# A DLRM forward pass on one core: MLP layers a pair per round ahead, the last pair gathered by halves, nine by-hand pairs

## The chip, the core and the metric

The kernel runs on one core of a Trainium2 chip. The metric is the device time of one launch in microseconds (us), the median of three runs. The core has five engines that run their own instruction streams and meet at semaphores: PE (matrix products; PEld is its weight load), DVE (vector work), ACT (scalar work, here mostly a DMA queue), POOL (here it issues the gathers) and SP (a DMA queue).

## The reference, cut to what matters

There are 2048 samples, 13 dense features, 26 tables of 12500 rows of 64 float32, an MLP 13-512-256-64 and a last layer of 256 outputs.

```python
x = jax.nn.relu(dense_features @ W0 + b0)
x = jax.nn.relu(x @ W1 + b1)
dense_out = jax.nn.relu(x @ W2 + b2)
emb = jax.vmap(lambda t, idx: t[idx], in_axes=(0, 1), out_axes=1)(tables, sparse_features)
gram = jnp.einsum('bid,bjd->bij', emb, emb)
interact = gram[:, TRIU_I, TRIU_J]
features = jnp.concatenate([dense_out, interact], axis=1)
return features @ Wt + bt
```

An index is clamped to its table (and a negative one wraps) before it is used.

## The kernel before

**Tiling.** The samples are cut into 32 units of 64, and two units (u = 0, 1) make a pair of 128 samples; there are 16 pairs, m = 0 to 15. Two pairs are a round (8 rounds), and the MLP is computed once per round on 256 samples.

**Gathers (POOL, `gather`, L276).** A gather is one indirect DMA of 128 rows of 256 bytes: two neighbouring fields (slot k of 13) of the 64 samples of one unit. A pair has 13 slots in two units, 26 gathers, in four chunks of 4, 4, 4 and 1 slots (`CHUNKS`). `emb` holds three pairs (`PR = 3`), so the gathers of pair m wait until the transposes of pair m-3 are done.

**By-hand rows (`fetch_rows`, L209).** In the eight pairs of `BY_HAND` one slot (`HAND_K` = 11) isn't gathered by POOL: its 256 rows are fetched by as many plain DMAs of one row each, those of unit 0 on SP's queue and those of unit 1 on ACT's, 32 at a time after a load of 32 row offsets into registers (a "piece"). SP fetches pair after pair. ACT has its pieces in a fixed order with the stores of the outputs in between: `store(done)` stands ahead of piece `done * 7 // 3 + 6` and waits for that output.

**A pair on PE and DVE.** PE transposes each chunk's rows (`transposes`, L506), DVE copies them to `embT` (`embT_evac`, L354). PE then makes the products of 4 samples at a time in two halves of 16 matmuls (`gram_products`, L524), into one PSUM tile, so that a half must be copied out (`gram_blocks`, L361, 16 copies of DVE) before the next is written. `top` (L542) multiplies the MLP's output and the products by the last layer's weights, DVE copies the result (`out_evac`, L391), and ACT stores it. In the last pair half of the 16 copies of a half are ACT's (`ACT_BLOCKS`).

**The order** is written out by hand, in `tensor_round` (L557) and `vector_round` (L398). In a round r the first layer (`mlp_l0`) stands behind the products of pair 2r, the second and third (`mlp_l1`, `mlp_l2`) between and behind the products of pair 2r+1. In the last round all three layers and `top(14)` stand ahead of the transposes of pair 15:

```python
                    mlp_l1(r)
                    mlp_l2(r)
                    top(2 * r)
                    transposes(2 * r + 1)
                    gram_products(2 * r + 1, 0)
                    gram_products(2 * r + 1, 1)
```

Of the kernel before, what the change touches and what calls it, by code (L numbers as in the profile page):

```python
# [5 lines left out]
def bass_dlrm_forward(  # L6
# [15 lines left out]
    i32 = mybir.dt.int32  # L22
# [38 lines left out]
    BY_HAND = [2, 4, 6, 8, 9, 11, 13, 15]  # L61
    HAND_K = 11
    LOADED = 32
    ROW = EMB * 4

# [19 lines left out]
    with ctx:  # L85
# [26 lines left out]
        row_idx = sb("row_idx", [P, NU, NK], u32)  # L112
        emb = sb("emb", [P, PR, NK, 2, EMB])
# [17 lines left out]
        h2 = sb("h2", [H2 + 1, RS])  # L131
# [14 lines left out]
        later_ready = sem("later_ready")  # L146
        hand_idx_in = sem("hand_idx_in")
# [47 lines left out]
        LAST_PAIR = NP - 1  # L195
# [69 lines left out]
        def _(pool):  # L265
# [29 lines left out]
            for m in range(NP):  # L295
                gather(m)

        @block.vector
        def _(dve):
# [49 lines left out]
            nc.vector.memset(h2[H2:H2 + 1, :], 1.0).then_inc(consts_set, 1)  # L349
            nc.vector.memset(w_tri[:, :, :], 0.0).then_inc(tri_zeroed, 1)  # L350
# [47 lines left out]
            def vector_round(r):  # L398
                embT_evac(2 * r)
                gram_blocks(2 * r, 0)  # L400
                if r > 0:
                    out_evac(2 * r - 1)
                gram_blocks(2 * r, 1)
                l0_evac(r)
                if r < ROUNDS - 1:
                    embT_evac(2 * r + 1)
                    gram_blocks(2 * r + 1, 0)
                    l1_evac(r)
                    gram_blocks(2 * r + 1, 1)
                    l2_evac(r)  # L410
                    out_evac(2 * r)
                else:
                    l1_evac(r)
                    l2_evac(r)
                    out_evac(2 * r)
                    embT_evac(2 * r + 1)
                    gram_blocks(2 * r + 1, 0)
                    gram_blocks(2 * r + 1, 1)

            dve.wait_ge(mlp_w_in, 96)  # L420
            for r in range(ROUNDS):
                vector_round(r)
# [3 lines left out]
        def _(act):  # L426
# [3 lines left out]
            with nc.allow_non_contiguous_dma(reason="bias columns"):  # L430
                act.dma_start(b0_sb[:, :], b0.rearrange("(c p) -> p c", p=P)).then_inc(mlp_w_in, 16)
                act.dma_start(b1_sb[:, :], b1.rearrange("(c p) -> p c", p=P)).then_inc(mlp_w_in, 16)
                act.dma_start(b2_sb[:, :], b2.rearrange("(p c) -> p c", c=1)).then_inc(mlp_w_in, 16)

# [12 lines left out]
            for i, (m, c0) in enumerate(pieces):  # L447
                for done in range(LAST_PAIR):
                    if done * 7 // 3 + 6 == i:
                        store(done)  # L450
                fetch_rows(act, 1, m, c0, c0 + LOADED)
            for done in range(LAST_PAIR):
                if done * 7 // 3 + 6 >= len(pieces):
                    store(done)
# [8 lines left out]
        def _(pe):  # L463
# [35 lines left out]
            def mlp_l2(r):  # L499
# [4 lines left out]
                last.then_inc(l2_in_psum, 1)  # L504

# [18 lines left out]
            def gram_products(m, half):  # L524
# [7 lines left out]
                pe.wait_ge(embT_ready[LAST], m + 1)  # L532
# [9 lines left out]
            def top(m):  # L542
                q = m % 2
                pe.wait_ge(h2_ready, m // 2 + 1)
                nc.tensor.matmul(mlp_ps[q][:, 0:NO], h2[:, q * P:(q + 1) * P], wd_sb[:, :], start=True, stop=False)  # L545
# [11 lines left out]
            def tensor_round(r):  # L557
                transposes(2 * r)
                gram_products(2 * r, 0)
                if r > 0:  # L560
                    top(2 * r - 1)
                gram_products(2 * r, 1)
                mlp_l0(r)
                if r < ROUNDS - 1:
                    transposes(2 * r + 1)
                    gram_products(2 * r + 1, 0)
                    mlp_l1(r)
                    gram_products(2 * r + 1, 1)
                    mlp_l2(r)
                    if r == 0:  # L570

                        pe.wait_ge(w_top_in, 96)
                        pe.wait_ge(tri_zeroed, 1)
                    top(2 * r)
                else:
                    mlp_l1(r)
                    mlp_l2(r)
                    top(2 * r)
                    transposes(2 * r + 1)
                    gram_products(2 * r + 1, 0)  # L580
                    gram_products(2 * r + 1, 1)

            for r in range(ROUNDS):
                tensor_round(r)
# [28 lines left out]
```

## Time and profile before

| | us |
|---|---|
| median of 3 runs (lowest, highest) | 541.34 (540.68, 541.42) |
| the profiled execution, own time | 541.29 |
| its span in the trace | 539.5 |
| PE busy in the span | 296.8 |
| DVE busy | 255.4 |
| POOL busy | 378.7 |

The profiled execution lies within the three runs; what lies around its span is 1.8 us. An engine's busy time counts only what its unit works, not what its sequencer does: POOL's gaps between two gathers are time in which nothing is waited for.

### The profile page before, as it was taken

The page shows a single profiled execution, that of the slowest core. Times are in us where ns is not written, and L with a number is a line of the kernel's source. Part 1 is how long each engine was busy: PE and PEld are TensorE (multiplying, and loading weights), DVE is VectorE, ACT ScalarE, POOL GpSimd, SP SyncE. Part 2 cuts the span into 40 slices and gives each one's busy share as a digit, 9 for nine tenths or more (in the row PEclk, how much of TensorE's full clock was granted, in tenths as well). Part 3 has the DMA queues.
Part 4 walks back from the last instruction along what each step waited for, and adds up shares of the span by engine and source line. Part 5 has one row for each costly group of instructions (what it writes and reads, how often), then busy time and mean ns, then how long its engine had stood idle before and what let it go on. Part 6 is the DMA issues. An engine that isn't in the chain of part 4 may idle for free.

```text
span 539.5 us, 8990 instructions
## 1 busy us (share of the span) xinstructions
PE 296.8 (55%) x1728; PEld 236.3 (44%) x1728; DVE 255.4 (47%) x656; ACT 8.7 (2%) x21; POOL 378.7 (70%) x407
## 2 busy tenths in 40 slices
PE   2015545861867517574366927529176381858666
PEld 1014334750645416463344815428064261647455
DVE  4404618471545716346182454525554273555442
ACT  2000000000000000000000000000000000000011
POOL 5777777777777777777777777777777777777300
PEclk9555558865576757767587666777577675878696
DMA  5212224122222223233232323232232322222000
GB/s 104 29 28 30 32 48 88 39 28 37 30 29 39 27 29 39 29 37 30 38 30 28 37 28 39 30 38 29 28 38 29 39 29 37 30 37 37 15 11 11
DMA packets 24758, 18.73 MB, mean 35 GB/s; under 512 B 14455, under 2 KB 18265, under 8 KB 24684
## 3 DMA queue, kind: packets, MB, share of 16 engines
q0 software_dynamic: 12800, 13.13, 17.6%
q1 hardware_dynamic: 6356, 2.49, 4.3%
q10 hardware_dynamic: 5546, 2.53, 4.1%
q14 instruction: 42, 0.34, 0.2%
q8 instruction: 14, 0.23, 0.2%
HBM read 15.20 MB, written 2.10 MB: 32 GB/s over the span
## 4 chain that ended last, share of the span: by engine, by line
POOL 61%; issue 21%; PE 7%; DVE 6%; DMA 3%; ACT 0%; POOLq 0%; DVEq 0%; ACTq 0%
POOL emb L288 61%; DVE gram L203 4%; PE gram_ps L538 3%; DMA emb<-in_L_rec_tables_dram,row_idx 3%; PE mlp_ps L553 2%; DVE embT L188 1%; PE mlp_ps L495 1%; DVE h L371 1%; DMA raw_idx<-n_r_sparse_features_dram 0%; ACT gram L203 0%; PE mlp_ps L545 0%; DVE out_sb L396 0%; PE rowsT_ps L520 0%; PE mlp_ps L502 0%; DVE wrap L315 0%
## 5 line engine op out<-in xcount | busy, mean ns | idle before, releaser
L288 POOL DMA_INDIRECT emb<-in_L_rec_tables_dram,row_idx x400 | 378.0, 945 | 125.6 <-issue 121.8
L203 DVE COPY gram<-gram_ps 32x96 f32<-32x96 f32 x496 | 161.0, 325 | 96.0 <-PE gram_ps L538 88.2
L520 PE MATMUL rowsT_ps<-ident,emb 128*128 128x128 f32 x200 | 43.7, 349 | 163.2 <-DMA emb<-in_L_rec_tables_dram,row_idx 160.2
L538 PE MATMUL gram_ps<-embT 64*128 64x100 f32 x1024 | 92.8, 350 | 29.3 <-DVE gram L203 17.1
L520 PEld LDWEIGHTS rowsT_ps<-ident,emb 128*128 128x128 f32 x200 | 28.7, 174 | 179.3 <-issue 178.5
L188 DVE COPY embT<-rowsT_ps 128x512 f32<-128x512 f32 x64 | 52.5, 851 | 115.3 <-PE rowsT_ps L520 114.4
L538 PEld LDWEIGHTS gram_ps<-embT 64*128 64x128 f32 x1024 | 86.9, 259 | 38.5 <-issue 38.5
L553 PE MATMUL mlp_ps<-w_gram,gram 128*128 128x256 f32 x224 | 75.9, 512 | 1.7 <-DVE gram L203 1.7
L553 PEld LDWEIGHTS mlp_ps<-w_gram,gram 128*128 128x128 f32 x224 | 61.8, 276 | 17.0 <-DVE gram L203 2.4
L495 PE MATMUL mlp_ps<-h,w_sb 128*128 128x256 f32 x128 | 38.9, 470 | 3.5 <-DVE h L371 3.5
L545 PE MATMUL mlp_ps<-wd_sb,h 65*128 65x256 f32 x32 | 17.9, 660 | 35.7 <-DVE h L371 35.7
L495 PEld LDWEIGHTS mlp_ps<-h,w_sb 128*128 128x128 f32 x128 | 30.3, 244 | 10.8 <-DVE h L371 4.2
L396 DVE COPY out_sb<-mlp_ps 128x256 f32<-128x256 f32 x16 | 6.8, 425 | 55.7 <-PE mlp_ps L553 55.4
L371 DVE TENSOR_SCALAR h<-mlp_ps,b_sb 128x256 f32<-128x256 f32 (+1 forms) x56 | 24.1, 477 | 7.8 <-PE mlp_ps L495 5.9
L545 PEld LDWEIGHTS mlp_ps<-wd_sb,h 65*128 65x128 f32 x32 | 7.4, 287 | 40.6 <-DVE h L371 33.9
L487 PE MATMUL mlp_ps<-xT,w_sb 13*128 13x256 f32 x64 | 21.3, 485 | 0.0
L487 PEld LDWEIGHTS mlp_ps<-xT,w_sb 13*128 13x128 f32 x64 | 14.5, 237 | 3.6 <-issue 0.5
L203 ACT COPY gram<-gram_ps 32x96 f32<-32x96 f32 (+1 forms) x16 | 5.2, 322 | 516.7 <-PE gram_ps L538 516.5
L502 PE MATMUL mlp_ps<-h,w_sb 128*64 128x256 f32 x32 | 8.6, 392 | 1.0 <-DVE h L371 1.0
L472 PE MATMUL rowsT_ps<-ident,x_sb 128*13 128x128 f32 x16 | 3.6, 412 | 5.6 <-DMA x_sb<-in_r_dense_features_dram 5.6
L350 DVE MEMSET w_tri<- 32x6400 f32 x1 | 5.4, 5392 | 1.4 <-issue 1.4
L502 PEld LDWEIGHTS mlp_ps<-h,w_sb 128*64 128x64 f32 x32 | 3.7, 136 | 3.3 <-DVE h L371 1.4
(25 smaller groups left out, 17.3 us busy)
## 6 DMA issues: line engine op xcount, KB each, us to landing
by_hand<-in_L_rec_tables_dram SPq DMA_DIRECT2D x1024, 0.2 KB
by_hand<-in_L_rec_tables_dram ACTq DMA_DIRECT2D x1024, 0.2 KB
emb<-in_L_rec_tables_dram,row_idx POOLq DMA_INDIRECT x400, 3.4
out_dram<-out_sb ACTq DMA_DIRECT2D x16, 128.0 KB, 6.7
w_gram<-w_tri SPq DMA_DIRECT2D x3, 192.0 KB
w_sb<-in_L_rec_W_dram SPq DMA_DIRECT2D x1, 512.0 KB
raw_idx<-n_r_sparse_features_dram SPq DMA_DIRECT2D x2, 182.0 KB, 4.1
w_gram<-w_tri SPq DMA_DIRECT2D x1, 224.0 KB
```

The lines of the kernel that those rows point to most:

```text
L188: return copy(embT[:, m % 2, :, 0:F].rearrange("p s (k x) -> p k x s", x=2)[:, ks.start:ks.stop], rowsT_ps[c % 2][:, 0:len(ks)])
L203: last = copy(by_quad[FP * g:FP * (g + 1), t0:NS, :, half * HG:(half + 1) * HG, s], gram_ps[FP * s:FP * (s + 1), :, :, src:src + SQ * (NS ...
L288: nc.gpsimd.indirect_dma_start(emb[:, m % PR, k, u, :], None, tables_v[:, :], bass.IndirectOffsetOnAxis(ap=row_idx[:, 2 * m + u, k:k + 1], ...
L371: return nc.vector.tensor_scalar(out, in_, bias, 0.0, ALU.add, ALU.max)
L396: nc.vector.tensor_copy(out_sb[:, q, :], mlp_ps[q][:, 0:NO]).then_inc(out_ready[q], 1)
L487: last = nc.tensor.matmul(mlp_ps[half][:, m * RS:(m + 1) * RS], w0_sb[:, c * P:(c + 1) * P], xT[:, bass.ds(r * 2, 2), :], start=True, stop ...
L495: last = nc.tensor.matmul(mlp_ps[0][:, m * RS:(m + 1) * RS], w1_sb[:, c, m * P:(m + 1) * P], h0[:, c, :], start=(c == 0), stop=(c == H0 // ...
L502: last = nc.tensor.matmul(mlp_ps[1][0:H2, 0:RS], w2_sb[:, c, :], h1[:, c, :], start=(c == 0), stop=(c == H1 // P - 1))
L520: last = nc.tensor.transpose(rowsT_ps[c % 2][:, k - ks.start, :, :], rows.rearrange("p u e -> p (u e)"), ident[:, :])
L538: last = nc.tensor.matmul(gram_ps[:, u, a, 0:SQ * (F - 1)], samples.rearrange("p s f -> p (s f)"), samples[:, :, 1:F], start=True, stop=True)
L545: nc.tensor.matmul(mlp_ps[q][:, 0:NO], h2[:, q * P:(q + 1) * P], wd_sb[:, :], start=True, stop=False)
L553: last = nc.tensor.matmul(mlp_ps[q][:, 0:NO], gram[:, q, t, :], w_gram[:, t, :], start=False, stop=(t == NS - 1))
```

## The change

1. The MLP of all rounds moves forward and stands in one piece: round 0's ahead of pair 0, and round m+1's behind the products of pair m, for m = 0 to 6. `h2` holds all rounds. The zeroing of `w_tri` (5.4 us on DVE) moves behind the first MLP.
2. The last pair is gathered otherwise: four fields of 32 samples in a gather, so that the first 12 gathers hold the first half of each unit's samples and the next 12 the second half. Its indices come by eight small DMAs on ACT's queue at the start and 14 small DVE operations behind pair 1. Transposes, copies and products of the first half stand ahead of those of the second.
3. Groups of 4, 3 and 5 spare products on PE, which nobody reads, stand between the last pair's steps.
4. Nine by-hand pairs in place of eight, at other places, with slot 12 in place of 11; for the last pair the by-hand rows are a chunk of their own (`None`), the third of six. A store stands one piece later on ACT's queue.

```diff
-    BY_HAND = [2, 4, 6, 8, 9, 11, 13, 15]
-    HAND_K = 11
+    BY_HAND = [2, 4, 5, 7, 9, 10, 12, 14, 15]
+    HAND_K = NK - 1
+    LAST_PAIR = NP - 1
+    LK = 2 * HAND_K // SQ
+    HS = US // 2
+    LAST_CHUNKS = [(0, 0, 4), (0, 4, LK), None, (1, 0, 4), (1, 4, 5), (1, 5, LK)]
+    HALF_DONE = [3, 6]
+    SPARE = [4, 3, 5]
...
+        def last_rowsT_evac(copy, i):
+            if LAST_CHUNKS[i] is None:
+                return copy(embT[:, LAST_PAIR % 2, :, 2 * HAND_K:F].rearrange("p s x -> p x s"),
+                            rowsT_ps[i % 2][:, 0, :, :])
+            half, k0, k1 = LAST_CHUNKS[i]
+            return copy(embT[:, LAST_PAIR % 2, half * HS:(half + 1) * HS, SQ * k0:SQ * k1].rearrange(
+                            "p s (k x) -> p k x s", x=SQ),
+                        rowsT_ps[i % 2][:, 0:k1 - k0].rearrange("p k y (x s) -> p k (y x) s", s=HS))
...
-            for m in range(NP):
+            for m in range(LAST_PAIR):
                 gather(m)
+            pool.wait_ge(rowsT_in_psum[LAST], LAST_PAIR + 1 - PR)
+            pool.wait_ge(last_idx_ready, 1)
...
+                for k in range(k0, k1):
+                    for u in range(2):
+                        nc.gpsimd.indirect_dma_start(
+                            emb[:, LAST_PAIR % PR, half * LK + k, u, :], None, tables_v[:, :],
+                            bass.IndirectOffsetOnAxis(ap=last_idx[:, half * 2 + u, k:k + 1], axis=0),
+                        ).then_inc(last_rows_in[i], 16)
...
             dve.wait_ge(mlp_w_in, 96)
-            for r in range(ROUNDS):
-                vector_round(r)
+            mlp_evac(0)
+            nc.vector.memset(w_tri[:, :, :], 0.0).then_inc(tri_zeroed, 1)
+            for m in range(LAST_PAIR):
+                embT_evac(m)
+                gram_blocks(m, 0)
+                if m > 0:
+                    out_evac(m - 1)
+                gram_blocks(m, 1)
+                if m + 1 < ROUNDS:
+                    mlp_evac(m + 1)
+                if m == 1:
+                    last_index()
+            dve.wait_ge(gram_in_psum, (LAST_PAIR - 1) * 2)
+            for i in range(HALF_DONE[0]):
+                dve.wait_ge(last_rowsT_in_psum, i + 1)
+                last_rowsT_evac(nc.vector.tensor_copy, i).then_inc(last_embT_ready, 1)
+            out_evac(LAST_PAIR - 1)
+            gram_blocks(LAST_PAIR, 0)
+            for i in range(HALF_DONE[0], HALF_DONE[1]):
+                dve.wait_ge(last_rowsT_in_psum, i + 1)
+                last_rowsT_evac(nc.vector.tensor_copy, i).then_inc(last_embT_ready, 1)
+            gram_blocks(LAST_PAIR, 1)
             out_evac(LAST_PAIR)
...
+            for x in range(SQ):
+                for a in range(2):
+                    act.dma_start(last_raw[x * HS:(x + 1) * HS, 2 * a:2 * a + 2, :],
+                                  sparse_v[a * HS:(a + 1) * HS, :, LAST_PAIR, :]).then_inc(last_idx_in, 16)
...
-                    if done * 7 // 3 + 6 == i:
+                    if done * 7 // 3 + 7 == i:
...
+            def spare(n):
+                pe.wait_ge(out_ready[(LAST_PAIR - 1) % 2], (LAST_PAIR - 1) // 2 + 1)
+                for _ in range(n):
+                    nc.tensor.matmul(mlp_ps[(LAST_PAIR - 1) % 2][:, 0:NO], ident[:, :], w_gram[:, 0, :], start=True, stop=True)
```

`last_transposes(i)` transposes chunk i of `LAST_CHUNKS` (for `None` the by-hand rows) into `rowsT_ps[i % 2]` once its rows have landed and the copy of chunk i-2 is done.

**PE at the end.** Before, from the products of pair 14's second half to the end of the program; L487, L495 and L502 are the MLP's layers, L545 and L553 are `top`, L520 transposes, L538 products:

```order
156 L538 MATMUL gram_ps<-embT 128x100 x16
157 L487 MATMUL mlp_ps0<-xT,w0_sb 128x256 x2
158 L487 MATMUL mlp_ps1<-xT,w0_sb 128x256 x2
159 L495 MATMUL mlp_ps0<-h0,w1_sb 128x256 x8
160 L502 MATMUL mlp_ps1<-h1,w2_sb 64x256 x2
161 L545 MATMUL mlp_ps0<-wd_sb,h2 128x256
162 L553 MATMUL mlp_ps0<-w_gram,gram 128x256 x7
163 L520 MATMUL rowsT_ps_0<-ident,emb 128x128 x4
164 L520 MATMUL rowsT_ps_1<-ident,emb 128x128 x4
165 L520 MATMUL rowsT_ps_0<-ident,emb 128x128 x3
166 L520 MATMUL rowsT_ps_0<-ident,by_hand 128x128
167 L520 MATMUL rowsT_ps_1<-ident,emb 128x128
```

In the changed kernel, from the same products on (L597 are the last pair's transposes, L605 spare products, L650 and L658 `top`, L642 products):

```order
153 L642 MATMUL gram_ps<-embT 128x100 x16
154 L597 MATMUL rowsT_ps_0<-ident,emb 128x128 x4
155 L597 MATMUL rowsT_ps_1<-ident,emb 128x128 x2
156 L650 MATMUL mlp_ps0<-wd_sb,h2 128x256
157 L658 MATMUL mlp_ps0<-w_gram,gram 128x256 x7
158 L597 MATMUL rowsT_ps_0<-ident,by_hand 128x128
159 L642 MATMUL gram_ps<-embT 128x100 x16
160 L597 MATMUL rowsT_ps_1<-ident,emb 128x128 x4
161 L605 MATMUL mlp_ps0<-w_gram,ident 128x256 x4
162 L597 MATMUL rowsT_ps_0<-ident,emb 128x128
163 L605 MATMUL mlp_ps0<-w_gram,ident 128x256 x3
164 L597 MATMUL rowsT_ps_1<-ident,emb 128x128
```

The MLP is gone from between pair 14 and pair 15, the transposes of the first half stand ahead of `top(14)`, and the by-hand chunk, behind `top(14)`, is ahead of the first half's products. Behind these rows stand the second half's products, five spare ones and `top(15)`.

**ACT at the end.** Before, the last pieces (L213 loads 32 offsets, L219 fetches 32 rows) and stores (L441):

```order
80 L441 DMA out_0_dram<-out_sb 128x256
81 L213 TENSOR_LOAD hand_off
82 L219 DMA by_hand<-in_L0_rec_tables_dram 1x256 x32
83 L213 TENSOR_LOAD hand_off
84 L219 DMA by_hand<-in_L0_rec_tables_dram 1x256 x32
85 L441 DMA out_0_dram<-out_sb 128x256
86 L213 TENSOR_LOAD hand_off
87 L219 DMA by_hand<-in_L0_rec_tables_dram 1x256 x32
88 L441 DMA out_0_dram<-out_sb 128x256 x3
```

In the changed kernel (L242, L248 and L514 are the same three):

```order
88 L514 DMA out_0_dram<-out_sb 128x256
89 L242 TENSOR_LOAD hand_off
90 L248 DMA by_hand<-in_L0_rec_tables_dram 1x256 x32
91 L242 TENSOR_LOAD hand_off
92 L248 DMA by_hand<-in_L0_rec_tables_dram 1x256 x32
93 L242 TENSOR_LOAD hand_off
94 L248 DMA by_hand<-in_L0_rec_tables_dram 1x256 x32
95 L514 DMA out_0_dram<-out_sb 128x256
96 L242 TENSOR_LOAD hand_off
97 L248 DMA by_hand<-in_L0_rec_tables_dram 1x256 x32
98 L514 DMA out_0_dram<-out_sb 128x256 x2
```

There are 36 pieces in place of 32, and 13 stores stand ahead of the last piece in both; two stores in place of three follow it.

## Rows read from the trace of the kernel before

**Rows 1.** The page: shares of the chain that ended last.

```profile
POOL 61%; issue 21%; PE 7%; DVE 6%; DMA 3%; ACT 0%; POOLq 0%; DVEq 0%; ACTq 0%
```

**Rows 2.** The chain's end in order of time: start, us, what.

```profile
441.86 16.20 DMA emb<-in_L_rec_tables_dram,row_idx
...
502.44 1.67 DVE h L371 x4
```

**Rows 3.** Groups of instructions, and POOL's last gather: start, us, idle before.

```profile
L288 POOL DMA_INDIRECT emb<-in_L_rec_tables_dram,row_idx x400 | 378.0, 945 | 125.6 <-issue 121.8
...
504.26 0.94 POOL L288 DMA_INDIRECT emb<-in_L_rec_tables_dram,row_idx  x1 [0.30 <-issue]
```

**Rows 4.** Gathers' landing in windows 90:100, 225:260, 320:360, 433:443, 463:475.

```profile
DMA to landing us min/median/max: 2.9/3.0/3.1
DMA to landing us min/median/max: 3.3/7.3/8.0
DMA to landing us min/median/max: 3.4/8.8/14.2
DMA to landing us min/median/max: 3.4/9.8/16.2
DMA to landing us min/median/max: 2.7/2.7/2.8
```

**Rows 5.** SP's and ACT's queues in order of time: start, us, what.

```profile
88.36 351.51 SPq L219 DMA_DIRECT2D by_hand<-in_L_rec_tables_dram  x896
...
4.38 0.50 ACTq L433 DMA_DIRECT2D b_sb<-in_L_rec_b_dram  x1
...
12.83 78.82 ACTq L219 DMA_DIRECT2D by_hand<-in_L_rec_tables_dram  x192
...
100.31 0.39 ACTq L441 DMA_DIRECT2D out_dram<-out_sb  x1
...
130.46 23.91 ACTq L219 DMA_DIRECT2D by_hand<-in_L_rec_tables_dram  x64
...
162.14 0.38 ACTq L441 DMA_DIRECT2D out_dram<-out_sb  x1
...
446.59 0.38 ACTq L441 DMA_DIRECT2D out_dram<-out_sb  x1
...
449.49 10.53 ACTq L219 DMA_DIRECT2D by_hand<-in_L_rec_tables_dram  x32
```

**Rows 6.** PE and DVE in order of time: start, us, shapes, idle before and releaser.

```profile
448.79 1.08 PE L520 MATMUL rowsT_ps<-ident,emb 128*128 128x128 f32 x4 [6.12 <-DMA emb<-in_L_rec_tables_dram,row_idx]
...
449.91 1.01 DVE L188 COPY embT<-rowsT_ps 128x512 f32<-128x512 f32 x1 [1.66 <-PE rowsT_ps L520]
...
459.15 3.74 PE L538 MATMUL gram_ps<-embT 64*128 64x100 f32 x32 [0.51 <-DVE embT L188]
...
468.57 2.03 PE L538 MATMUL gram_ps<-embT 64*128 64x100 f32 x32 [1.60 <-DVE gram L203]
...
470.71 5.37 DVE L203 COPY gram<-gram_ps 32x96 f32<-32x96 f32 x16 [1.38 <-PE gram_ps L538]
...
477.66 4.74 PE L553 MATMUL mlp_ps<-w_gram,gram 128*128 128x256 f32 x14
...
512.96 3.19 PE L553 MATMUL mlp_ps<-w_gram,gram 128*128 128x256 f32 x14
...
522.09 2.64 DVE L203 COPY gram<-gram_ps 32x96 f32<-32x96 f32 x8 [2.24 <-PE gram_ps L538]
...
525.11 3.73 PE L538 MATMUL gram_ps<-embT 64*128 64x100 f32 x32 [3.13 <-ACT gram L203]
...
531.71 5.09 PE L553 MATMUL mlp_ps<-w_gram,gram 128*128 128x256 f32 x14 [1.71 <-DVE gram L203]
...
536.84 0.42 DVE L396 COPY out_sb<-mlp_ps 128x256 f32<-128x256 f32 x1 [5.20 <-PE mlp_ps L553]
```

**Rows 7.** Window 525.2:535.3: length, busy PE, PEld, DVE, ACT, POOL; granted clock, DMA, GB/s.

```profile
525.20:535.30 10.10, 8.39 (x43) 6.76 (x44) 2.59 (x8) 2.60 (x8) 0.00 (x0) 0.50 0.01 2
```

More of the change, by code:

```diff
@@ L146, in bass_dlrm_forward @@
         later_ready = sem("later_ready")
+        last_idx_in = sem("last_idx_in")
+        last_idx_ready = sem("last_idx_ready")
+        last_rows_in = [sem(f"last_rows_in_{i}") for i in range(len(LAST_CHUNKS))]
+        last_rowsT_in_psum = sem("last_rowsT_in_psum")
+        last_embT_ready = sem("last_embT_ready")
         hand_idx_in = sem("hand_idx_in")
@@ L420, in _, with mlp_evac, last_index @@
-            dve.wait_ge(mlp_w_in, 96)
-            for r in range(ROUNDS):
-                vector_round(r)
+            def mlp_evac(r):
+                l0_evac(r)
+                l1_evac(r)
+                l2_evac(r)
+            def last_index():
+                dve.wait_ge(last_idx_in, 128)
+                for x in range(SQ):
+                    rows, raw = slice(x * HS, (x + 1) * HS), last_raw[x * HS:(x + 1) * HS, :, x:SQ * LK:SQ]
+                    nc.vector.tensor_scalar(last_wrap[rows], raw, 0.0, float(VOCAB), ALU.is_lt, ALU.mult)
+                    last = nc.vector.tensor_scalar(last_capped[rows], raw, float(VOCAB - 1), None, ALU.min)
+                last.then_inc(hand_idx_step, 1)
+                dve.wait_ge(hand_idx_step, 4)
+                nc.vector.tensor_tensor(last_wrapped[:, :, :], last_capped[:, :, :], last_wrap[:, :, :],
+                                        ALU.add).then_inc(hand_idx_step, 1)
+                dve.wait_ge(hand_idx_step, 5)
+                nc.vector.scalar_tensor_tensor(
+                    out=last_row[:, :, :], in0=last_wrapped[:, :, :], scalar=0.0,
+                    in1=field_base[:, :, 0:2 * LK:2].to_broadcast([P, 4, LK]), op0=ALU.max,
+                    op1=ALU.add).then_inc(hand_idx_step, 1)
+                dve.wait_ge(hand_idx_step, 6)
+                for x in range(SQ):
+                    rows = slice(x * HS, (x + 1) * HS)
+                    last = nc.vector.tensor_scalar(last_idx[rows], last_row[rows], float((x - x // 2) * VOCAB), None,
+                                                   ALU.add)
+                last.then_inc(last_idx_ready, 1)
@@ L504, in mlp_l2, with last_transposes @@
                 last.then_inc(l2_in_psum, 1)
+            def last_transposes(i):
+                if LAST_CHUNKS[i] is None:
+                    for u in range(2):
+                        pe.wait_ge(by_hand_in[BY_HAND.index(LAST_PAIR)][u], 16 * P)
+                    rows = [by_hand[:, BY_HAND.index(LAST_PAIR), :, :]]
+                else:
+                    half, k0, k1 = LAST_CHUNKS[i]
+                    pe.wait_ge(last_rows_in[i], 16 * 2 * (k1 - k0))
+                    rows = [emb[:, LAST_PAIR % PR, half * LK + k, :, :] for k in range(k0, k1)]
+                if i < 2:
+                    pe.wait_ge(embT_ready[i + 2], LAST_PAIR)
+                else:
+                    pe.wait_ge(last_embT_ready, i - 1)
+                nc.tensor.nop(nofuse=True)
+                for n, row in enumerate(rows):
+                    last = nc.tensor.transpose(rowsT_ps[i % 2][:, n, :, :], row.rearrange("p u e -> p (u e)"),
+                                               ident[:, :])
+                last.then_inc(last_rowsT_in_psum, 1)
+            def spare(n):
+                pe.wait_ge(out_ready[(LAST_PAIR - 1) % 2], (LAST_PAIR - 1) // 2 + 1)
+                for _ in range(n):
+                    nc.tensor.matmul(mlp_ps[(LAST_PAIR - 1) % 2][:, 0:NO], ident[:, :], w_gram[:, 0, :], start=True, stop=True)
             def transposes(m):
@@ L555, in top, with mlp @@
                 last.then_inc(top_in_psum[q], 1)
[L557 to L562, printed above, removed]
-                mlp_l0(r)
[L564 to L584, printed above, removed]
+            def mlp(r):
+                mlp_l0(r)
+                mlp_l1(r)
+                mlp_l2(r)
+            mlp(0)
+            for m in range(LAST_PAIR):
+                transposes(m)
+                gram_products(m, 0)
+                if m == 1:
+                    pe.wait_ge(w_top_in, 96)
+                    pe.wait_ge(tri_zeroed, 1)
+                if m > 0:
+                    top(m - 1)
+                gram_products(m, 1)
+                if m + 1 < ROUNDS:
+                    mlp(m + 1)
+            last_transposes(0)
+            last_transposes(1)
+            top(LAST_PAIR - 1)
+            last_transposes(2)
+            gram_products(LAST_PAIR, 0)
+            last_transposes(3)
+            spare(SPARE[0])
+            last_transposes(4)
+            spare(SPARE[1])
+            last_transposes(5)
+            gram_products(LAST_PAIR, 1)
+            spare(SPARE[2])
             top(LAST_PAIR)
```

54 lines of the change are left out of this document (24 added, 30 removed).

## The prediction

> **What bounds the kernel now.** I read the page's last chain first, then that chain in order of time, then the landing of the gathers window by window, the two DMA queues, and the last 100 us of PE and DVE. Of the chain, 61% is POOL's gathers and 21% "issue", POOL's own gaps between them [rows 1]: 400 gathers at 945 ns with a gap of 0.30, or 1.249 us each, with nothing waited for [rows 3]. But POOL isn't what ends the program. Its last gather is issued at 504.26 [rows 3], and the span ends at 539.5. The chain leaves POOL at 441.86, with pair 13's last gather, whose rows are 16.20 us on their way [rows 2]; from their landing at 458.1 on it is PE and DVE taking turns through pairs 13 and 14, the last round's MLP and pair 15. Of that the MLP alone holds the stretch from 502.44 [rows 2] to the products of `top(14)` at 512.96 [rows 6], 10.5 us, at a time when pair 15's rows have long landed.
>
> The second thing to see is that 16.20 us. A gather's slowest rows take 3.1 us at 90 to 100, 8.0 at 225 to 260, 14.2 at 320 to 360, 16.2 at 433 to 443, and 2.8 again from 463 on; the quickest take 3.4 all the while [rows 4]. So one part of the DMA work falls behind, and a chunk waits for its slowest row. The lateness grows while SP and ACT both fetch by-hand rows; SP ends at 439.87 and ACT at 460.0 [rows 5], and by 463 it is gone: 13.4 us back in 21, some of it with ACT still at work. I conclude that by-hand rows and one share of each gather stand in one line. This is inferred: no row shows the DMA engine.
>
> The Trainium skill has a rule on this, in "DMA: Bandwidth & Descriptors", section "Why a DMA increments its semaphore by 16 and not by 1": a DMA from SP or ACT that can't be split runs on the lowest-numbered of the 16 DMA engines. By that rule all 2304 by-hand rows of the changed kernel queue on one engine, each beside the gathers' share there; spread over 16, they would leave the case without lateness below. The trace agrees as far as it goes, with 3.4 and 16.2 us in one window [rows 4].
>
> **The change part by part.**
>
> *POOL.* Eight of the first 15 pairs are by hand: 15 x 26 - 16 = 374 gathers; the last pair has 24. That is 398, two fewer: the last is issued at 504.26 - 2 x 1.249 = 501.8, pair 14's last at 501.8 - 24 x 1.249 = 471.8. The gathers of the last pair are as large as others; I take the same price.
>
> *MLP ahead.* Off the tail go 10.5 us. It costs in the first pairs: a pair with MLP on one chain is about 18 us (transposes and copies 2.4, products and copies 9.4 + 7.5, worked out below) plus some 14 us of layers and their copies, near the 31.2 us (25 gathers) that POOL needs for a pair. So PE may slip by 1 to 4 us a pair, some 20 us in all by pair 7, and gains 13 a pair afterwards. What hides it is `emb` with three pairs: POOL waits only when PE is two pairs, 62 us, behind. Above that each us would be POOL's. I count 0. The `w_tri` zeroing behind the first MLP ends near 40, while SP only comes to need it after its first 128 by-hand rows at 61: 0. The index work for the last pair (14 small DVE operations) hides in the same slack, and is wanted at 471.8 at the earliest.
>
> *ACT's queue.* Eight more DMA issues at the start, at 0.50 us by the bias issue [rows 5], put ACT's first piece from 12.83 to about 17. A piece costs 13.6 us at the start (six in 78.82 and one more load of 2.6) and 13.4 with a store at the end, so some 12.6 without [rows 5]; I take 13.2. The bounds shift ACT's end by 22 us down or 14 up, but a faster ACT makes the line of rows longer by as much work, so that its last row lands at nearly the same time. Thirty-six pieces and 13 stores (0.8 each) end at 17 + 475 + 10 = 502, the last row issued at 499.5. SP's pairs cost 351.51 + 2.6 over 7 = 50.6, so eight of them from 88.36 end at 490.5. In the kernel before, ACT stood still for its stores, as from 91.65 to 100.31 and from 154.37 to 162.14 [rows 5], 16.4 us; behind it, the lateness fell to 3.1 [rows 4]. With a store a piece later I expect these pauses gone.
>
> *The lateness, carried on.* Two bounds. Level: it stays at 16.2, as from 349 to 442 it grew by 2.0 only. Steep: 0.067 us per us, as from 257 to 349 (8.0 to 14.2, [rows 4]), for the 49 us from 442 on, and 16.4 us of pauses that no longer give back 0.45 each (from 441.9 to 472 at most, 13.4 us in 30): 16.2 + 3.3 + 7.4 = 27. I take 23: the pauses' 7.4 less the part that the floor of 2.8 would have cut off, and little growth after. From SP's end at 490.5 it falls at 0.45.
>
> *Pair 14.* Its last gather lands at 471.8 + 23 = 494.8. Four transposes 1.08, their copy 1.01, a by-hand chunk and the waits make 2.4 [rows 6]: 497.2. From the first half's products to the second's 9.4 (459.15 to 468.57), from there to the end of its copies 7.5 (470.71 + 5.37): 514.1. `top(14)`, after PE has idled, 4.74 [rows 6]: 518.9. The last pair's first transposes lie beside this.
>
> *The by-hand chunk of pair 15.* ACT's last row, issued at 499.5, is late by 23 - 9 x 0.45 = 19: it lands at 518.5. PE's in-order queue has it ahead of the first half's products, so nothing of the last pair is multiplied earlier. The last gather, at 501.8, is late by about 18 and lands near 520, which the second half's transposes need only from 522 on. The halves thus start when everything is there.
>
> *From 518.9 to the end.* Transpose, copy and wait 0.9: 519.8. Products 2.03 and copies by DVE and ACT 2.64 [rows 6]: 524.6. Copy of the second half's four slots 1.01, the last transpose and copy 0.7: 526.3. Products 2.03, copies 2.68: 531.1. Five spares are ten passes at 3.19/14 = 0.23, and with `top`'s first product 0.7 they end at 531.4, 0.3 past the copies. `top` 3.19, the output's copy 0.5, and 2.24 from there to the span's end, as before (537.26 to 539.5) [rows 6]: 537.3.
>
> *The spares* are counted in that: before, PE's clock stood at 0.50, the 1.2 GHz level, from 525.2 to 535.3 [rows 7], after PE had idled for 3.1 us, and the second products took 3.73 and `top` 5.09, against 2.03 and 3.19 at the upper level [rows 6]. If PE is at the lower level all through, the tail is longer by 1.7 + 1.7 + 1.9 and by 1.5 for spares in the way: 6.8. If they are no help nor harm, by 3.6.
>
> **Sum.** A span of 537.3 against 539.5, -2.2, or 541.29 - 2.2 = **539.1 us** on the profiled execution's own time, 0.05 under the median of the runs. What a change in the tail could have won, some 14 us, is given back to rows that land late.
>
> **The rivals.**
>
> *No lateness to speak of (the by-hand rows find room).* All is in 2.8 us after its issue. Last gather 504.6, ACT's last row 502.3: the tail is that from 518.9, 18.4 us, behind 504.6, or 523. Time 525. For it: [rows 4] show the lateness gone within 25 us. Against it: the fetch now runs to 499.5 and not to 460.
>
> *The lateness levels off at 16.2.* Pair 14 lands at 488 and is through `top(14)` by 512; ACT's last row lands at 499.5 + 12 = 511.7: span 530.5, time 532. For it, the 2.0 us of growth in the last 92; against it, that ACT's early pauses had let it start from 3.1 at 90 to 100.
>
> *Slower: the line grows as in its steep stretch.* Place: pair 14's last gather. At 27 us it lands 4 later, and ACT's last row is as late: span 541.3, time 543; with PE at the lower level through the tail up to 6.8 more. It decides from 26.3 on, where the 2.2 us won and the 1.1 of the measurement's limit are used up. For it, the loss of ACT's pauses; against it, the slow growth behind 349.
>
> *The change doesn't do what it says,* in that the halves win nothing: that is my forecast's own mechanism. If PE loses more in the first pairs than three buffers hide, POOL would wait; for that the slip would have to be three times my estimate. At 20 us past the 62 it is 559; I give it 2 in 100.
>
> **Numbers.** A difference under 0.2%, 1.1 us, can't be told from none. Chances: forecast's case 53, level 13, no lateness 9, slower 23, POOL held up 2. The likeliest case's own range is 536.5 to 542 (lateness 20.5 to 26). The range reaches from below the level case to the bound of the slower one: 530 to 544.5. Faster: 22 from the two better cases and 34 of the forecast's 53, 56. Same: 18 of the 53. Slower: the last 1 and the 25 of the two others, 26.
>
> **What the profile would show.** If I'm right: gathers still 1.249 us apart to 501.8; slowest landings of 20 us and over between 440 and 490; PE's pair 14 transposes near 495, waiting for a gather; the by-hand transpose at 518 or later; second products of pair 15 at 2.03. The prediction is wrong if landings near 470 take less than 16 us (faster), if they take over 26, if PE in the tail is at the lower level (slower), or if POOL shows a wait.

## The result, and the profile after

| | us |
|---|---|
| before, median of 16 runs (lowest, highest) | 541.37 (540.35, 542.87) |
| changed, median of 16 runs (lowest, highest) | 543.63 (541.73, 544.9) |
| ratio, 95% interval | 1.004 (1.003 to 1.0051) |
| changed, the profiled execution: own time, span | 543.01, 541.2 |

The change makes the kernel slower by 0.4%, where I had forecast 539.1 us and a small gain. The time lies in the range; the sign is wrong.

The page of the changed kernel, its chain that ended last, and POOL's group of gathers:

```profile
ACTq 52%; issue 13%; SPq 10%; DMA 9%; PE 8%; DVE 7%; DVEq 0%
...
L317 POOL DMA_INDIRECT emb<-in_L_rec_tables_dram,row_idx x374 | 353.1, 944 | 117.6 <-issue 113.9
```

POOL, 61% of the chain before [rows 1], is not in it any more. The chain now goes through ACT's queue and its by-hand rows. POOL itself is unchanged: 944 ns a gather, and nearly all its idle time is its own gaps, so the MLP ahead never held it up.

SP's and ACT's queues in order of time (start, us, what):

```profile
90.75 402.50 SPq L248 DMA_DIRECT2D by_hand<-in_L_rec_tables_dram  x1024
...
486.74 10.90 ACTq L248 DMA_DIRECT2D by_hand<-in_L_rec_tables_dram  x32
```

SP ends at 493.25 and ACT at 497.64, against 439.87 and 460.0 before [rows 5]. Next the gathers' landing in the windows 433:443 and 500:503 (shortest, median and longest of those gathers for which the trace has a landing):

```profile
DMA to landing us min/median/max: 3.4/12.0/20.7
DMA to landing us min/median/max: 3.4/11.6/19.8
```

The slowest rows take 20.7 us (16.2 before) and still 19.8 at the last gathers, where the kernel before was back at 2.8 from 463 on [rows 4]. The chain names the longest wait behind ACT's last row (start, us):

```profile
497.40 23.64 DMA by_hand<-in_L_rec_tables_dram
```

PE, DVE and POOL in order of time (start, us, shapes, idle before and releaser):

```profile
492.94 1.08 PE L621 MATMUL rowsT_ps<-ident,emb 128*128 128x128 f32 x4 [11.24 <-DMA emb<-in_L_rec_tables_dram,row_idx]
...
501.46 0.94 POOL L336 DMA_INDIRECT emb<-in_L_rec_tables_dram,last_idx  x1 [0.30 <-issue]
...
512.39 4.97 PE L658 MATMUL mlp_ps<-w_gram,gram 128*128 128x256 f32 x14 [4.29 <-DVE gram L232]
...
521.13 0.30 PE L597 MATMUL rowsT_ps<-ident,by_hand 128*128 128x128 f32 x1 [3.77 <-DMA by_hand<-in_L_rec_tables_dram]
...
521.94 3.12 PE L642 MATMUL gram_ps<-embT 64*128 64x100 f32 x32 [0.51 <-DVE embT L219]
...
530.07 2.03 PE L642 MATMUL gram_ps<-embT 64*128 64x100 f32 x32 [0.67 <-DVE embT L222]
...
534.99 3.26 PE L658 MATMUL mlp_ps<-w_gram,gram 128*128 128x256 f32 x14
...
538.29 0.42 DVE L438 COPY out_sb<-mlp_ps 128x256 f32<-128x256 f32 x1 [3.38 <-PE mlp_ps L658]
```

PE gets pair 14's last chunk at 492.94, is through `top(14)` at 517.4 and then stands still for 3.77 us, until the by-hand rows of pair 15 land at 521.1. Everything of the last pair's products is behind that transpose in PE's queue. The windows 518:521.4 and 521.4:525.2 (length; busy PE, PEld, DVE, ACT, POOL; granted clock, DMA, GB/s):

```profile
518.00:521.40 3.40, 0.27 (x1) 0.14 (x1) 0.00 (x0) 0.00 (x0) 0.00 (x0) 1.00 0.02 2
521.40:525.20 3.80, 3.29 (x34) 3.11 (x34) 0.65 (x3) 0.04 (x1) 0.00 (x0) 0.67 0.10 35
```

After the idle stretch the clock falls to 0.67 on average, between the 1.2 and 2.4 GHz levels, and the first half's products take 3.12 us where the second's take 2.03.

### The profile page after: what moved, and what is told of

The parts are those of the page before. It is cut to its first block, busy times and chain, and to the rows that moved or that the text cites. A ratio compares the mean times of both kernels' runs of the same rounds, so it can differ in the third digit from the quotient of the medians.

```text
span 541.2 us, 9582 instructions
## 1 busy us (share of the span) xinstructions
PE 303.3 (56%) x1752; PEld 240.6 (44%) x1752; DVE 258.0 (48%) x672; ACT 8.8 (2%) x21; POOL 376.6 (70%) x405
## 3 DMA queue, kind: packets, MB, share of 16 engines
q1 hardware_dynamic: 6612, 2.52, 5.3%
## 4 chain that ended last, share of the span: by engine, by line
ACTq 52%; issue 13%; SPq 10%; DMA 9%; PE 8%; DVE 7%; DVEq 0%
ACTq L248 40%; ACTq L242 11%; SPq L248 6%; DMA by_hand<-in_L_rec_tables_dram 4%; DVE gram L232 4%; DMA w_tri<-in_L_rec_Wt_dram 3%; PE gram_ps L642 3%; PE mlp_ps L569 2%; PE mlp_ps L658 2%; SPq L242 2%; DMA w_gram<-w_tri 1%; SPq L281 1%; DVE h L413 1%; DMA raw_idx<-n_r_sparse_features_dram 1%; DVE embT L209 1%
## 5 line engine op out<-in xcount | busy, mean ns | idle before, releaser
L317 POOL DMA_INDIRECT emb<-in_L_rec_tables_dram,row_idx x374 | 353.1, 944 | 117.6 <-issue 113.9
L621 PE MATMUL rowsT_ps<-ident,emb 128*128 128x128 f32 x187 | 37.1, 333 | 134.8 <-DMA emb<-in_L_rec_tables_dram,row_idx 127.5
L642 PE MATMUL gram_ps<-embT 64*128 64x100 f32 x1024 | 91.3, 345 | 27.5 <-DVE gram L232 14.4
L642 PEld LDWEIGHTS gram_ps<-embT 64*128 64x128 f32 x1024 | 85.3, 254 | 37.0 <-issue 37.0
L621 PEld LDWEIGHTS rowsT_ps<-ident,emb 128*128 128x128 f32 x187 | 24.6, 166 | 146.4 <-issue 145.7
L209 DVE COPY embT<-rowsT_ps 128x512 f32<-128x512 f32 (+1 forms) x60 | 47.7, 851 | 85.5 <-PE rowsT_ps L621 85.1
L658 PE MATMUL mlp_ps<-w_gram,gram 128*128 128x256 f32 x224 | 70.1, 481 | 4.4 <-DVE gram L232 4.3
L569 PE MATMUL mlp_ps<-h,w_sb 128*128 128x256 f32 x128 | 48.7, 561 | 32.6 <-DVE h L413 32.6
L658 PEld LDWEIGHTS mlp_ps<-w_gram,gram 128*128 128x128 f32 x224 | 57.5, 258 | 17.8 <-DVE gram L232 5.2
L569 PEld LDWEIGHTS mlp_ps<-h,w_sb 128*128 128x128 f32 x128 | 37.1, 297 | 45.4 <-DVE h L413 37.0
L336 POOL DMA_INDIRECT emb<-in_L_rec_tables_dram,last_idx x24 | 22.7, 944 | 7.3 <-issue 7.3
L561 PE MATMUL mlp_ps<-xT,w_sb 13*128 13x256 f32 x64 | 23.0, 518 | 1.4 <-DVE h L392 1.4
L650 PE MATMUL mlp_ps<-wd_sb,h 65*128 65x256 f32 x32 | 16.7, 619 | 12.5 <-DMA w_gram<-w_tri 12.5
L650 PEld LDWEIGHTS mlp_ps<-wd_sb,h 65*128 65x128 f32 x32 | 7.1, 272 | 14.9 <-DMA w_gram<-w_tri 12.7
L545 PE MATMUL rowsT_ps<-ident,x_sb 128*13 128x128 f32 x16 | 3.7, 412 | 9.1 <-DMA x_sb<-in_r_dense_features_dram 5.7
```

Source lines behind the costliest of these rows:

```text
L209: return copy(embT[:, m % 2, :, 0:F].rearrange("p s (k x) -> p k x s", x=2)[:, ks.start:ks.stop], rowsT_ps[c % 2][:, 0:len(ks)])
L317: nc.gpsimd.indirect_dma_start(emb[:, m % PR, k, u, :], None, tables_v[:, :], bass.IndirectOffsetOnAxis(ap=row_idx[:, 2 * m + u, k:k + 1], ...
L569: last = nc.tensor.matmul(mlp_ps[0][:, m * RS:(m + 1) * RS], w1_sb[:, c, m * P:(m + 1) * P], h0[:, c, :], start=(c == 0), stop=(c == H0 // ...
L621: last = nc.tensor.transpose(rowsT_ps[c % 2][:, k - ks.start, :, :], rows.rearrange("p u e -> p (u e)"), ident[:, :])
L642: last = nc.tensor.matmul(gram_ps[:, u, a, 0:SQ * (F - 1)], samples.rearrange("p s f -> p (s f)"), samples[:, :, 1:F], start=True, stop=True)
L650: nc.tensor.matmul(mlp_ps[q][:, 0:NO], h2[:, m // 2, q * P:(q + 1) * P], wd_sb[:, :], start=True, stop=False)
```

## The experiments

My theory after the result: the by-hand rows hold up the end in two ways, through the gathers that they delay and through pair 15's own by-hand chunk, and the ninth pair is what makes both last to the end. Rivals: that the MLP ahead, the halves or the spare products cost the time; that only pair 14's late gathers count; and that the by-hand rows stand in a line of their own, apart from the gathers.

**Eight by-hand pairs.** All else as changed.

```diff
-    BY_HAND = [2, 4, 5, 7, 9, 10, 12, 14, 15]
+    BY_HAND = [2, 4, 6, 8, 9, 11, 13, 15]
```

> The changed kernel with the eight by-hand pairs of before (2, 4, 6, 8, 9, 11, 13, 15), all else kept. If the nine pairs' rows, which stand in one line and land up to 24 us after their issue, take the gain away (theory), SP is through near 442 and ACT near 450, the slowest landings are back at 2.8 us from about 470 on, POOL's last gather at 504.3 lands at 507.1, and some 12 to 18 us of last products, copies and top follow: 520 to 527 us. If the new order itself costs on PE and DVE, or the halves give nothing (rival), it stays at 535 us or over.

Measured: 528.17 us (527.94 to 529.04), ratio to before 0.9745 (0.9729 to 0.9761), a little over the 520 to 527 that I expected; the rival's 535 or more is out. The chain, SP's and ACT's queues, and the landing in the window 463:475:

```profile
441.50 20.61 DMA emb<-in_L_rec_tables_dram,row_idx
```

```profile
90.90 351.70 SPq L248 DMA_DIRECT2D by_hand<-in_L_rec_tables_dram  x896
...
420.17 23.94 ACTq L248 DMA_DIRECT2D by_hand<-in_L_rec_tables_dram  x64
```

```profile
DMA to landing us min/median/max: 2.7/2.7/2.8
```

At 441.5 the slowest row takes 20.61 us, as in the changed kernel. But SP ends at 442.6 and ACT at 444.1, and from 463 on the gathers counted land in 2.8 us. PE in order of time:

```profile
485.77 3.74 PE L642 MATMUL gram_ps<-embT 64*128 64x100 f32 x32 [1.13 <-DVE embT L209]
...
503.00 5.66 PE L658 MATMUL mlp_ps<-w_gram,gram 128*128 128x256 f32 x14 [4.32 <-DVE gram L232]
...
508.50 0.27 PE L597 MATMUL rowsT_ps<-ident,by_hand 128*128 128x128 f32 x1
...
509.29 2.03 PE L642 MATMUL gram_ps<-embT 64*128 64x100 f32 x32 [0.51 <-issue]
...
524.52 0.42 DVE L438 COPY out_sb<-mlp_ps 128x256 f32<-128x256 f32 x1 [3.38 <-PE mlp_ps L658]
```

`top(14)` ends 8.7 us earlier (503.00 + 5.66 against 512.39 + 4.97), the by-hand transpose follows without the 3.8 us of wait for a DMA, and the first products take 1.1 less: 13.6 of the 14.0 us by which the span is shorter. The median falls by 15.5 (16.0 by the ratios, each to the kernel before on its chip). The ninth pair costs the change its whole gain. The two lists differ in places as well as in number, and nine pairs at other places weren't run; but SP needs 0.39 us a row with either list (402.50 for 1024, 351.70 for 896), so its end goes with the number of rows.

**Fewer still: seven and six pairs.** The lists are `[2, 4, 6, 8, 10, 12, 15]` and `[2, 4, 6, 9, 12, 15]`.

> The changed kernel with seven by-hand pairs (2, 4, 6, 8, 10, 12, 15). With eight the tail was still a chain of PE and DVE from pair 13, whose rows landed 20.6 us late; with seven the fetch is through near 395 and the line gone by 420, so pair 14 is through top(14) near 503 and POOL's last gather, 2.5 us later, lands near 509: 522 to 526 us, 2 to 6 less than with eight. If POOL alone counted by then (rival), 2.5 us more than with eight: 530.7.

> Six by-hand pairs (2, 4, 6, 9, 12, 15). If with seven POOL sets the end, two more gathers add 2.5 us to the time of seven: 525 to 528 us. If the line of rows still costs with seven, six is the same or less.

Measured: seven 525.01 us (524.1 to 525.38), ratio 0.9709 (0.9693 to 0.9725); six 526.47 (525.99 to 528.27), ratio 0.9741 (0.972 to 0.9762). Both as expected. With seven, the chain's step before pair 14's products, and POOL's last gather:

```profile
477.23 2.72 DMA emb<-in_L_rec_tables_dram,row_idx
```

```profile
507.23 0.94 POOL L336 DMA_INDIRECT emb<-in_L_rec_tables_dram,last_idx  x1 [0.30 <-issue]
```

The last gather of pair 14 now lands in 2.72 us, so what is left is POOL's own rate: each by-hand pair given up should cost two gathers, 2.5 us. From nine to eight the time falls by 15.5 us, from eight to seven by 3.2 (1.9 by the ratios, as the two ran on different chips), and from seven to six it rises by 1.5 (the profiled spans, 521.9 and 524.8, by 2.9). Seven pairs is the fastest version here, 3% under the kernel before.

**Nine pairs alone.** The kernel before, with only the nine pairs, their slot and the later stores.

```diff
-    BY_HAND = [2, 4, 6, 8, 9, 11, 13, 15]
-    HAND_K = 11
+    BY_HAND = [2, 4, 5, 7, 9, 10, 12, 14, 15]
+    HAND_K = NK - 1
...
-                    if done * 7 // 3 + 6 == i:
+                    if done * 7 // 3 + 7 == i:
```

> The kernel before with the nine by-hand pairs, slot 12 and the later stores alone. Theory: pair 14's rows land near 493 and the by-hand rows of pair 15 near 521, and since the last round's MLP and top(14) stand ahead of pair 15, its transposes begin near 530: 550 to 556 us. Rival (fewer gathers are what counts): 2.5 us less than before, 539 us.

Measured: 551.18 us (549.97 to 551.54), ratio 1.0163 (1.0147 to 1.018), as expected. In its chain:

```profile
472.51 20.12 DMA emb<-in_L_rec_tables_dram,row_idx
...
512.18 1.67 DVE h L371 x4
```

Pair 14's last gather is 20.12 us on its way, and the last round's MLP starts at 512.18 in place of 502.44 [rows 2]: 9.7 us, which is the loss of 9.2 beside the kernel before (541.93) on that chip.

**The MLP ahead alone.** The changed kernel with the last pair gathered as before, no spare products, eight pairs, slot 11 and the stores at their old places:

```diff
-            for m in range(LAST_PAIR):
+            for m in range(NP):
...
-            last_transposes(0)
-            last_transposes(1)
-            top(LAST_PAIR - 1)
-            last_transposes(2)
...
-            spare(SPARE[2])
```

> The kernel before with the MLP a pair per round ahead alone: eight by-hand pairs, slot 11, the last pair gathered and multiplied as any other (top(14) between its halves), no spares. Theory: POOL's last gather at 504.3 lands at 507.1 and 20 to 24 us of two products, two copies and top follow: 528 to 533 us. Rival (PE and DVE fall behind in the first pairs and POOL waits, or the MLP of the last round was hidden anyway): 539 us or more.

Measured: 538.1 us (536.61 to 539.32), ratio 0.9937 (0.9913 to 0.9961): a gain, but some 5 us short of what I expected. In order of time:

```profile
507.68 3.74 PE L608 MATMUL gram_ps<-embT 64*128 64x100 f32 x32 [0.51 <-DVE embT L209]
...
511.52 2.66 DVE L232 COPY gram<-gram_ps 32x96 f32<-32x96 f32 x8 [3.95 <-PE gram_ps L608]
...
512.36 4.11 PE L624 MATMUL mlp_ps<-w_gram,gram 128*128 128x256 f32 x14
516.50 0.42 DVE L424 COPY out_sb<-mlp_ps 128x256 f32<-128x256 f32 x1 [2.32 <-PE mlp_ps L624]
516.96 0.34 ACTq L483 DMA_DIRECT2D out_dram<-out_sb  x1
517.69 2.63 ACT L232 COPY gram<-gram_ps 32x96 f32<-32x96 f32 x8 [507.88 <-DVE out_sb L424]
520.43 3.22 PE L608 MATMUL gram_ps<-embT 64*128 64x100 f32 x32 [3.96 <-issue]
```

ACT is in order: its share of the last pair's copies stands behind the store of pair 14, which waits for DVE's copy at 516.50. DVE's half starts at 511.52, ACT's at 517.69, 6.2 us later. PE is busy with `top(14)` up to 516.47 and then stands still for 3.96 us until ACT's copies are done at 520.32: so much of the time goes to a store that nothing waits for. The changed kernel has `top(14)` ahead of the last pair's products and avoids this. With eight pairs, the halves, the spares and the rest bring 538.1 down to 528.2.

**Without spare products,** once with nine pairs and once with eight.

```diff
-    SPARE = [4, 3, 5]
+    SPARE = [0, 0, 0]
```

> The changed kernel without the spare products (0, 0, 0). If they hold PE's clock at its upper level in the tail, the second half's products go from 2.03 to 3.7 us and top's 14 passes from 3.26 to about 5.1, while 0.3 us of spares in the way are saved: 546.5 us (2.5 to 3.5 more). If the clock stays up without them (rival), 543.3 us or a little less.

> Eight by-hand pairs without the spare products. As with nine, PE's clock falls in the tail: 2.5 to 3.7 us more than the 528.2 of eight with them, 531 to 532 us. Rival: no difference, 528.

Measured: nine 547.29 us (546.86 to 547.87), ratio 1.0096 (1.008 to 1.0113), 3.7 us more than with them and near what I expected; eight 534.18 (532.75 to 535.13), ratio 0.9882 (0.9865 to 0.9898), 6.0 more, which is over what I expected. By the ratios, each to the kernel before on its chip, it is 3.0 and 7.4, by the profiled spans 4.9 (546.1 and 541.2) and 3.7 (530.9 and 527.2). Windows from the last pair's first products to the output's copy, of the changed kernel, nine without spares, eight with and eight without (columns as above):

```profile
521.90:538.30 16.40, 15.54 (x110) 13.24 (x110) 7.08 (x21) 5.28 (x16) 0.00 (x0) 0.90 0.03 9
```

```profile
522.40:543.50 21.10, 15.43 (x86) 12.53 (x86) 7.32 (x21) 5.22 (x16) 0.00 (x0) 0.54 0.02 7
```

```profile
509.30:524.50 15.20, 14.12 (x110) 11.69 (x110) 7.01 (x20) 5.29 (x16) 0.00 (x0) 1.00 0.03 10
```

```profile
508.60:528.30 19.70, 13.85 (x86) 10.98 (x86) 6.97 (x21) 5.24 (x16) 0.00 (x0) 0.65 0.02 7
```

PE's real work takes longer without the spares: the clock stands at 0.54 in place of 0.90, and 0.65 in place of 1.00. The spares are a gain in both; in which it is larger isn't shown, as the times and the traces disagree.

**A shorter end of the by-hand rows.** The changed kernel, with the last 32 rows of each unit of pair 15 brought by two transfers of 16 neighbouring rows.

```diff
             for c0 in range(first, stop, LOADED):
+                if m == LAST_PAIR and c0 == P - LOADED:
+                    for x in range(2):
+                        p0, n = x * US + c0 // 2, LOADED // 2
+                        eng.dma_start(by_hand[p0:p0 + n, i, u, :].bitcast(mybir.dt.uint8),
+                                      tables_bytes[0:n * ROW].rearrange("(p e) -> p e", p=n)
+                                      ).then_inc(by_hand_in[i][u], 16)
+                    continue
...
-                        pe.wait_ge(by_hand_in[BY_HAND.index(LAST_PAIR)][u], 16 * P)
+                        pe.wait_ge(by_hand_in[BY_HAND.index(LAST_PAIR)][u], 16 * (P - LOADED + 2))
```

> The changed kernel, but the last 32 rows of each sample half of pair 15's by-hand rows are not looked up: two transfers of 16 neighbouring rows each, from the start of the tables, take their place (so that share of the last pair's values is left out). SP's and ACT's streams then end some 12 and 10 us earlier, near 481 and 487. Theory 'by-hand rows of pair 15 set the end': they land at about 487 + 23.6 = 511, before they are wanted; pair 14's gathers (issued up to 471.5) are as late as in the changed kernel, 21 us, and pair 14's top products end near 517.4 as before; the last pair's by-hand transpose follows at about 518 without a wait, its first products take 2.0 to 2.3 us instead of 3.1, and the time falls by about 4 us, to 539 to 540. Rival 'it is pair 14 and the products behind it that set the end': the time stays within 1 us of the changed kernel's, 543 to 544.

Measured: 538.47 us (537.26 to 539.02), ratio 0.994 (0.992 to 0.9959), a profiled span of 537.2; a little under what I expected. The chain's wait for pair 14, and PE in order of time:

```profile
471.41 20.95 DMA emb<-in_L_rec_tables_dram,row_idx
```

```profile
512.74 5.96 PE L665 MATMUL mlp_ps<-w_gram,gram 128*128 128x256 f32 x14 [4.30 <-DVE gram L232]
518.53 0.27 PE L604 MATMUL rowsT_ps<-ident,by_hand 128*128 128x128 f32 x1
...
519.31 2.03 PE L649 MATMUL gram_ps<-embT 64*128 64x100 f32 x32 [0.51 <-issue]
```

Pair 14 is as late as ever, and `top(14)` ends a little later, at 518.7. The by-hand transpose follows at once, the products are back at 2.03, and the span is 4.0 shorter. So it is that one wait, with the slower products behind it, that makes the change slower than the kernel before; the rival that pair 14 sets the end alone is out.

**Without the last pair's gathers.** The changed kernel without its 24 last gathers.

```diff
-            for i, chunk in enumerate(LAST_CHUNKS):
...
-                        nc.gpsimd.indirect_dma_start(
-                            emb[:, LAST_PAIR % PR, half * LK + k, u, :], None, tables_v[:, :],
...
-                    pe.wait_ge(last_rows_in[i], 16 * 2 * (k1 - k0))
```

> The changed kernel without the 24 gathers of the last pair (its transposes read what pair 12 left in the same buffer, so the last pair's values are left out). The by-hand rows are issued as before, SP's up to 493 and ACT's up to 497.5. Theory 'by-hand rows and gathers are served by the same engine': from 472 on it has less to do, so pair 15's last by-hand rows take well under 20 us in place of 23.6 and land before 517; then the by-hand transpose waits no longer, pair 14's gathers are as late as before (21 us at 471.5), and the time falls by 3 to 5 us, to 538.5 to 540.5. Rival 'the by-hand rows have a line of their own that the gathers don't touch': they land at 521 as before, the transpose waits again for about 4 us, and the time stays at 543 to 544.5.

Measured: 538.95 us (537.78 to 543.69), ratio 0.9966 (0.9942 to 0.9991), as expected. ACT's last rows and PE:

```profile
485.79 10.94 ACTq L248 DMA_DIRECT2D by_hand<-in_L_rec_tables_dram  x32
...
516.97 0.27 PE L586 MATMUL rowsT_ps<-ident,by_hand 128*128 128x128 f32 x1
```

ACT ends at 496.7, 0.9 earlier than in the changed kernel, and the transpose runs at 516.97 without a wait for a DMA, 4.2 earlier: the rows landed at most 20.2 us behind ACT's end, against 23.5 (521.13 less 497.64). Gathers delay by-hand rows too; the rival of separate lines that don't touch is out.

**Rows in sixteen pieces.** I meant to spread a by-hand row over more DMA engines by writing both sides as 16 pieces of 16 bytes.

```diff
-                    eng.dma_start(by_hand[row:row + 1, i, u, :].bitcast(mybir.dt.uint8),
-                                  tables_bytes[bass.ds(off, ROW)].rearrange("(a e) -> a e", a=1)
+                    eng.dma_start(by_hand[row:row + 1, i, u, :].bitcast(mybir.dt.uint8).rearrange("a (b e) -> a b e", b=16),
+                                  tables_bytes[bass.ds(off, ROW)].rearrange("(a b e) -> a b e", a=1, b=16)
```

> The changed kernel, nine pairs, with each by-hand row fetched as 16 pieces of 16 bytes in one DMA, so that a row may spread over the DMA engines. If the line forms on one engine and a row's price there goes with its bytes, the late landings vanish and the end is POOL's: about 520 us. If a row's price goes with the number of pieces (theory, as 256 bytes are little), every engine now has what one had: the quickest landings are as late as the slowest (over 10 us in the second half), and the time is 543 us or more. If the rows had nothing to do with the lateness (rival), all stays: 543.6 us with landings from 3.4 to 21.

Measured: 544.28 us (543.91 to 544.61), the changed kernel's time. SP's queue on the page (packets, MB, share of 16 engines), of the changed kernel and then of this one:

```profile
q1 hardware_dynamic: 6612, 2.52, 5.3%
```

```profile
q1 hardware_dynamic: 6612, 2.52, 5.2%
```

The number of packets is the same, so the pieces must have been joined again: nothing was spread, and the run says nothing on what spreading would do. A layout whose pieces can't be joined wasn't tried.

## Why the prediction was wrong, step by step

**POOL: right.** Last gather 501.46, forecast 501.8.

**MLP ahead: nothing in the first pairs, right; 10.5 us off the tail, not shown by itself.** POOL's idle time is its own gaps. The MLP ahead alone gained 3.8 us (541.93 to 538.1), with ACT's store in its way. With eight pairs, the halves and the spares the time falls by 13.8 us (to 528.17), near the "some 14 us" that the prediction had for the tail.

**The queues' ends: near.** SP 493.25 for 490.5, ACT 497.64 for 502; the last row is issued at 497.4 for 499.5. Why the prediction has 2.5 us between that row and ACT's end it doesn't say; in the trace there are 0.24.

**Lateness of 23 at pair 14: near, and inside its bounds.** 492.94 for 494.8 at PE, and `top(14)` through at 517.4 for 518.9. The slower rival, the line's steep growth, did not happen: the longest landing is 20.7 us in the window 433:443 and 20.95 at 471.41 with the shorter end, so the lateness had levelled off, as another rival had it, but at 20 to 21 and not at 16.2.

**The by-hand chunk of pair 15: here the prediction failed.** It had "ACT's last row, issued at 499.5, is late by 23 - 9 x 0.45 = 19: it lands at 518.5", in time for PE. It landed at 521.0, 23.6 us after its issue, and PE went on at 521.1. So the issue was 2.1 us earlier than forecast and the lateness 4.6 larger. Two things in that lateness were wrong. The by-hand rows got the gathers' lateness, though they are later than these. And the fall of 0.45 us per us behind SP's end, 4 us in all, isn't to be seen. The gathers' landing in the windows 484:488 and 498:500:

```profile
DMA to landing us min/median/max: 3.4/3.4/20.2
DMA to landing us min/median/max: 3.4/11.5/19.7
```

From 20.2, ahead of SP's end at 493.25, it came to 19.8 for the last gather, issued 8.2 us behind that end; and the last by-hand row, issued 4.15 us behind it and not 9, still had 23.6. The prediction had the two ends of PE's wait 0.4 us apart (518.5 and 518.9) without making a rival of it, so 2.2 of the 2.6 us by which the landing was off went straight into the end.

That the measured time lies in the stated range is luck in part: it is outside the likeliest case's own 536.5 to 542, and near the 543 of the slower rival, which had it from pair 14.

**The tail: 18.4 forecast, 20.1 measured** from the by-hand transpose to the end. 1.1 of the 1.7 is the first half's products at 3.12 for 2.03: PE had idled in the wait that the forecast did not have, and the clock fell behind it.

The forecast span was 537.3, the measured one 541.2: 2.2 us by the start of the tail (521.1 for 518.9) and 1.7 within it. With the wait taken away (the shorter end) the span is 537.2.

**The spares: right.** Leaving them out costs 3.7 us with nine pairs (3.0 by the ratios); the forecast had 3.6 for spares that don't help.

**What the change would have been worth.** The prediction's sum said that late rows take back what the tail gains, and never asked what the change would be without the ninth pair; the runs show that this decides the sign. Nine alone cost 9.2 us, nearly all through pair 14 (9.7 on the chain). Nine in place of eight in the changed kernel cost 15.5: 8.7 of the span through pair 14, 3.8 through the wait for pair 15's by-hand rows and 1.1 through the clock behind it.

**What stays open.** Why by-hand rows are later than gathers issued behind them is not shown by any row here. The prediction had them in one line, but not in order of issue: the gather issued at 498.97 took 19.7 us and landed at 518.7, 2.4 us ahead of the by-hand row issued 1.6 us before it. The Trainium skill, "DMA: Bandwidth & Descriptors", section "Queues, rings and completion order", says that a DMA engine takes its queues in turn, a packet from each. By that rule a by-hand row waits for its own queue's backlog and a gather for POOL's, and one lateness for both, as I took it, is not to be had. The trace agrees as far as it goes: the last gather was issued at 501.46, 4.1 us after ACT's last row, and with the 19.8 of its window it lands at 521.3, as that row does at 521.0. The gathers' removal shortened the by-hand rows' wait, which fits as well. That one share of each gather is late and the rest quick, as the prediction read from the shortest landings, isn't shown either: 3.4 and 19.8 us in the window 500:503 are two gathers of one chunk, which count on one semaphore, so the 3.4 need not be a whole gather.

## What to carry to other kernels

Rows that were fetched one by one on two queues delayed the gathers beside them here, and the delay lasted some 20 us beyond the last issue (from ACT's end at 444.1 to a landing at 462.1 with eight pairs, from 497.4 to 521.0 with nine): count back from the end of the program to see when such a stream has to stop, and prefer the number of rows at which it stops before the last stage asks for its data. Take the lateness of a queue's own transfers from that queue, not from another beside it. Where two arrivals are forecast within a microsecond of each other ahead of a waiting engine, make each of them a case with its own price.

## What the runs showed of the hardware that was not expected

The lateness didn't go by how many rows are still to come: it is 20.6 us at 441.5 with eight pairs and 20.7 in the window 433:443 with nine. Nor did it grow from there on: with nine it is much the same near the end (20.95 for the gather at 471.41 with the shorter end, 19.8 for the last one). With eight, where SP ends at 442.6 and ACT at 444.1, it is gone in the window 463:475.

What differs at 441 is the kernel before, at 16.20 us [rows 2], and the MLP ahead alone:

```profile
441.36 18.05 DMA emb<-in_L_rec_tables_dram,row_idx
```

Both have eight pairs and the stores at their old places, against 20.61 with eight pairs and the stores a piece later. This fits the prediction's view that ACT's stops at its stores let the queue clear; but slot 11 and the start of ACT's queue differ too, and no run moved the stores by themselves.

A wait of 3.77 us cost more than itself: the products behind it ran 1.1 us longer at a mean clock of 0.67. With no such wait, at the same place in the kernel with eight pairs, the clock was 1.00 throughout, and with the shorter end of nine the products took 2.03.

Written-out pieces of a contiguous row leave the number of packets unchanged (6612 on SP's queue both times).
